# Causal attention with a quantised side product on one core: the order of a round's work changed on every engine

## The reference, cut to what matters

```python
xn = _layernorm(x)                                  # x: (4, 1024, 128)
q, k, v = (split_heads(xn @ W) for W in (Wq, Wk, Wv))   # 16 heads of 64
w = softmax(q @ k.T / 64 + causal)                  # 1024 x 1024 per head
mask = clip((arange(1024) + span * 1024) / 33, 0, 1)
w = w * mask; w = w / (sum(w) + 1e-8)
attn = concat_heads(w @ v) @ Wo
xi = clip(round(xn / scale), -127, 127) * scale     # made finite
out = x + attn + xi @ (ternary - 1).T + bias
```

## Time and profile before

| what | value |
|---|---|
| median of 3 runs | 1007.33 us (1005.56 to 1009.34) |
| the profiled execution | 1003.91 us, span 1002.2 us |
| granted TensorE clock | 0.997 of full speed |
| TensorE (PE) | 981.3 us busy, 98% |
| VectorE | 768.3 us, 77% |
| GpSimd | 708.8 us, 71% |
| ScalarE | 451.3 us, 45% |

### The profile page before, as it was taken

One profiled execution on the slowest core, in us unless ns is written; L12 is line 12 of the kernel. 1 busy time (PEld: TensorE's weight loads), 2 busy tenths in 40 slices (PEclk: granted clock), 3 DMA queues, 4 the chain that ended last, 5 costly groups with the idle time before them and its releaser, 6 DMA issues.

```text
span 1002.2 us, 19150 instructions
## 1 busy us (share of the span) xinstructions
PE 981.3 (98%) x7081; PEld 631.0 (63%) x7081; DVE 768.3 (77%) x1734; ACT 451.3 (45%) x607; POOL 708.8 (71%) x650
## 2 busy tenths in 40 slices
PE   7799999999999999999999999999999999999997
PEld 3566666666665666666666666666666666666654
DVE  8778888878788888877767877777877777787752
ACT  4344454444454444454444454444454443454442
POOL 8666767667767668767767777667767667767673
PEclk9999999999999999999999999999999999999999
DMA  6000000000000000000000000000000000000000
GB/s 176 3 3 2 2 1 3 2 2 3 1 23 2 3 2 3 1 3 2 3 12 12 2 3 2 2 3 2 2 2 24 2 3 2 1 2 2 2 1 22
DMA packets 16117, 8.52 MB, mean 9 GB/s; under 512 B 5388, under 2 KB 15628, under 8 KB 16024
## 3 DMA queue, kind: packets, MB, share of 16 engines
q1 hardware_dynamic: 15416, 7.16, 2.7%
q10 hardware_dynamic: 608, 0.14, 0.1%
HBM read 4.33 MB, written 2.10 MB: 6 GB/s over the span
## 4 chain that ended last, share of the span: by engine, by line
PE 88%; DVE 8%; issue 2%; DMA 1%; ACT 1%; SPq 0%; DVEq 0%; ACTq 0%
PE ring L939 25%; PE pv L956 25%; PE ring L912 12%; PE beside L995 7%; PE beside L968 6%; PE ring L885 3%; PE ring L881 3%; PE ring L882 3%; DVE ring L732 2%; DVE v L718 2%; PE ring L899 1%; DVE beside L756 1%; PE beside L983 1%; PE beside L919 1%; PE ring L900 1%
## 5 line engine op out<-in xcount | busy, mean ns | idle before, releaser
L541 ACT ACTIVATE prob<-ring 128x1024 f32<-128x1024 f32 (+3 forms) x384 | 293.6, 810 | 348.2 <-PE ring L939 348.2
L475 POOL TENSOR_TENSOR psumd<-psumd,prob 128x512 f32<-128x512 f32 (+1 forms) x252 | 410.7, 1630 | 28.7 <-ACT prob L541 0.8
L732 DVE CUSTOM_DVE_ANT_0 ring<-ring,causal 128x128 f32<-128x128 f32 (+3 forms) x512 | 240.3, 517 | 96.4 <-PE ring L912 96.0
L939 PE MATMUL ring<-q,k 64*128 64x512 f32 (+3 forms) x2304 | 280.0, 347 | 3.9 <-DMA mrow<-maxrow 2.4
L956 PE MATMUL pv<-prob,v 128*64 128x512 f32 (+3 forms) x1536 | 267.2, 490 | 0.0
L448 POOL TENSOR_SCALAR_AFFINE_SELECT prob<-prob 128x256 f32<-128x256 f32 x256 | 107.0, 419 | 218.0 <-ACT prob L541 215.8
L939 PEld LDWEIGHTS ring<-q,k 64*128 64x128 f32 x2304 | 195.2, 185 | 39.4 <-DVE rowmax L732 5.7
L956 PEld LDWEIGHTS pv<-prob,v 128*64 128x64 f32 x1536 | 104.7, 137 | 153.6 <-issue 139.9
L736 DVE TENSOR_REDUCE rowmax<-ring 128x2 f32<-128x1024 f32 x128 | 151.4, 1222 | 4.7 <-PE ring L912 1.4
L471 POOL TENSOR_TENSOR psumd<-prob 128x768 f32<-128x768 f32 x64 | 134.8, 2106 | 23.1 <-ACT prob L541 18.3
L912 PE MATMUL ring<-k,q 64*128 64x512 f32 (+3 forms) x768 | 143.2, 408 | 5.4 <-ACT k L530 1.2
(11 more groups left out here) (112 smaller groups left out, 942.4 us busy)
## 6 DMA issues: line engine op xcount, KB each, us to landing
x_sb<-in_L_attn_query SPq DMA_DIRECT2D x4, 512.0 KB, 5.2
kext<-kext SPq DMA_DIRECT2D x128, 4.0 KB, 1.7
out<-x_sb SPq DMA_DIRECT2D x8, 256.0 KB, 2.5
mrow<-maxrow SPq DMA_DIRECT2D x64, 4.0 KB
xn_sb<-in_L_attn_Wv SPq DMA_DIRECT2D x1, 512.0 KB, 5.2
wo<-in_L_attn_Wo SPq DMA_DIRECT2D x1, 512.0 KB, 7.3
xn_sb<-in_L_attn_Wq SPq DMA_DIRECT2D x1, 448.0 KB, 3.5
xn_sb<-in_L_attn_Wk SPq DMA_DIRECT2D x1, 448.0 KB, 4.2
```

The source lines that it names most:

```text
L475: g.tensor_tensor(acc[:, :, lo:HALF], acc[:, :, lo:HALF], pr[:, :, lo:HALF], ALU.add).then_inc(acc_done, 1)
L541: a.activation(prob[n % NPROB][:, :, lo:HALF], ring[:, slot(f"S{t}", i), :, lo:HALF], ACT.Exp, scale=1.0 / DH).then_inc(exp_done, 1)
L732: last = v.tensor_tensor_reduce(out=ring[:, s, h, 0:n], in0=ring[:, s, h, 0:n], in1=causal[:, HALF - n:HALF], scale=1.0, scalar=MASKED, op ...
L939: last = t_.matmul(ring[:, s, h, lo:HALF], k[p][rows, keys], q[p][rows, cols], start=(at == 0), stop=(at == len(parts) - 1))
```

## The change

All four engines' lists are written in another order. On TensorE, S0 and D1- and G11- now come in this sequence right behind the projections, and M0 and M1 behind them; Y0 moves into the next round and stands ahead of V, Y1 behind V; S7 and S8 come earlier. On VectorE the quantisation step q moves from the middle of the round to its start, ahead of Qlo and Klo, and one pair later; X0, X1 and W move ahead of R0 and R1. GpSimd's L and A are interleaved in another way, ScalarE's ln1-, ex1- stand behind E0. The last round has lists of its own for TensorE and now for VectorE.

```diff
-PE_PLAN = ("T Q+ K+ X0 X1 W G11- M0+ M1+ S0 S1 S2 M2+ D1- M3+ S3 V+ S4 S5 M4+ S6 M5+ Y1- M6+ M7+ S7 D0 G3 "
-           "M8+ S8 S9 S10 M9+ Y0 M10+ M11+ S11 G7")
+PE_PLAN = ("T Q+ K+ X0 X1 W S0 D1- G11- M0+ M1+ S1 S2 S3 S4 M2+ M3+ Y0- V+ Y1- M4+ S5 S6 S7 M5+ D0 M6+ M7+ "
+           "S8 G3 M8+ S9 M9+ S10 S11 M10+ M11+ G7")
...
-PE_LAST = "T G11- S0 S1 S2 D1- S3 S4 S5 Y1- S6 S7 D0 G3 S8 S9 S10 Y0 S11 F1 G7 D1 G11 Y1"
+PE_LAST = "T S0 D1- G11- S1 S2 S3 S4 Y0- S5 Y1- S6 S7 D0 G3 S8 S9 S10 Y0 S11 F1 G7 D1 G11 Y1"
...
     if name == "q":
-        return i % PAIRS_OF_BATCH < PAIRS_OF_BATCH - 1
+        return i % PAIRS_OF_BATCH > 0
...
-            for name, i in walk(DVE_PLAN, DVE_FIRST):
+            for name, i in walk(DVE_PLAN, DVE_FIRST, DVE_LAST):
...
-                    quantise(i // NPB, i % NPB + 1)
+                    quantise(i // NPB, i % NPB)
```

More of the change, by code:

```diff
@@ L25 @@
 LAST = N_PAIRS - 1
-PE_PLAN = ("T Q+ K+ X0 X1 W G11- M0+ M1+ S0 S1 S2 M2+ D1- M3+ S3 V+ S4 S5 M4+ S6 M5+ Y1- M6+ M7+ S7 D0 G3 "
-           "M8+ S8 S9 S10 M9+ Y0 M10+ M11+ S11 G7")
[L38 to L41, removed]
+PE_PLAN = ("T Q+ K+ X0 X1 W S0 D1- G11- M0+ M1+ S1 S2 S3 S4 M2+ M3+ Y0- V+ Y1- M4+ S5 S6 S7 M5+ D0 M6+ M7+ "
+           "S8 G3 M8+ S9 M9+ S10 S11 M10+ M11+ G7")
+ACT_PLAN = "Z Qhi+ Khi+ X0 X1 E0 ln1- ex1- E1 E2 E3 E4 E5 E6 E7 ln0 ex0 E8 E9 E10 E11"
+DVE_PLAN = ("Tc Z q Qlo+ Klo+ X0 X1 W R0+ R1+ t1- u1- o1- R2+ Ya0- R3+ Vs+ R4+ Ya1- R5+ R6+ R7+ t0 u0 R8+ "
+            "o0 R9+ R10+ R11+ Rc+")
+POOL_PLAN = "L0 L1 L2 A0 L3 A1 A2 A3 A4 A5 A6 A7 L8 L9 A8 L10 A9 A10 L11 A11 B"
 PE_FIRST = ("Q+ K+ M0+ M1+ M2+ I0+ M3+ I1+ M4+ I2+ M5+ I3+ M6+ I4+ M7+ I5+ M8+ M9+ M10+ M11+ Q++ T+ "
@@ L46 @@
 ACT_FIRST = "xf0+ Qhi+ xf1+ Khi+ rest+ keys+ wv+ Qhi++ Khi++ E0+ E1+ E2+"
-PE_LAST = "T G11- S0 S1 S2 D1- S3 S4 S5 Y1- S6 S7 D0 G3 S8 S9 S10 Y0 S11 F1 G7 D1 G11 Y1"
+PE_LAST = "T S0 D1- G11- S1 S2 S3 S4 Y0- S5 Y1- S6 S7 D0 G3 S8 S9 S10 Y0 S11 F1 G7 D1 G11 Y1"
+DVE_LAST = "Tc q t1- u1- o1- Ya0- Ya1- t0 u0 o0 Ya0 t1 u1 o1 Ya1"
 POOL_LAST = "L0 A0 L1 A1 L2 A2 L3 A3 A4 A5 A6 L8 L9 L10 A7 L11"
```

## The result

The changed kernel takes 1043.02 us in the median of 4 runs, the kernel before 1006.67 beside it. The ratio is 1.0367, with a 95% interval of 1.0343 to 1.0391: 36 us slower, where I had said 18 and a range up to 1034. The profiled execution took 1042.16 us, with a span of 1040.4. That span is 38.2 longer than before's, and this is the number that the trace can take apart.

The account below looks back on a forecast made before the run. TensorE, busy for 98% of the span, was taken as the bound. Plain rounds +9.6, D1 behind X +9.2, W in round 1 +1.1, early rounds -3.0 and ends +1.4 made +18.3 on 1007.33: 1025 us, range 1012 to 1034.

Parts of the forecast that it names:

- Switches: TensorE's changes of shape between units: 14 per round before, 11 after, saving 0.60 us per plain round.
- loads: TensorE weight loads not ahead of their unit, as behind a wait for a ring slot: 0.11 us more each.
- mrow: S0 follows the projections at once and waits for the two DMAs behind T: 0.36 us added per plain round.
- late slots: S2, S3, S4, S8, S10, S11 and M10 on TensorE get ring slots or loads late: 1.29 us added per plain round.
- plain round: A round without layer norm or X, T to T: 29.69 us before, 30.01 forecast, +9.6 in 30 rounds.
- the old waits: TensorE waits of M4, M2 and M9 in the old order that go: 0.73 us saved per plain round.
- rival 3: GpSimd's sums (A11) reach D1 late; ending 0.5 us late costs 15 over 30 rounds: 1040 us, chance 0.10.
- D1 behind X: In rounds 4, 5, 12, 13, 20 and 21 D1 waits for VectorE's read of X0 or X1: +9.2 us.
- The ends: Round 0 loses a Y0 (-1.1 us), the last round gains it and waits for mrow (+2.5): +1.4 together.
- Early rounds: Round 2 and five others with layer norm lose their wait for Klo, as units needing it stand later: -3.0 us.

## Why the prediction was wrong

The direction and the mechanisms that I had named were right, the size was half of what was measured, and a wait that I had not named made the most of the difference.

- **Switches, loads, mrow, late slots: right as a sum.** The plain round was 30.01 in the forecast. With Rc's wait taken away it measured 30.04 to 30.07. The waits for mrow and for the slots of S2 and S3 are there one by one, to 0.02 us. The savings of 0.60 for three switches and 0.73 for the old waits were not measured each by itself; that they are right is shown only by the sum.
- **The step that failed is the last one of the plain round.** I let T follow G7 at once and gave Rc no term. It took 1.35, and T waited: 0.40 in each of 30 rounds, 12 of the 20 us that were missing. I had placed GpSimd's sums only against D1 (rival 3, where they were in time, since A11 ended at T+2.9), and never against VectorE. The trace of the kernel before had the sign of it: a maximum over 8 numbers lasting 0.65 and ending with GpSimd's sum.

  The Trainium skill (SBUF — State Buffer, "SBUF: two separate sides") says that VectorE and GpSimd share a pair of ports of SBUF (the memory that holds these tensors) under an exclusive lock: of a VectorE instruction with two SBUF inputs and a GpSimd instruction that reads SBUF, the one that starts first has the pair for its whole length, and the other is blocked. The trace agrees: Rc with two inputs ends 0.02 behind the sum, wherever in the sum it started, and takes 0.17 where it meets none; Rc with one input takes 0.17 inside a sum.
- **D1 behind X: right in kind.** D1 came at T+6.1 in rounds 13, 20 and 21, against 6.06 forecast, at 6.3 and 6.55 in rounds 4 and 5, against 7.05 and about 6.4, but at 8.38 in round 12. In round 4 I had taken the 2.95 of the four normalisations from before as theirs, but part of it was a wait for GpSimd's sums; with the new order it is 2.23. Round 12 cost 5.9 instead of 2.5: the same meeting of VectorE and GpSimd, and then the clock, which had no term in the sum.
- **The ends: too small.** From the last T to the end it took 5.1 more, where I had 2.5, for the low clock behind the 3 us of idle time. Round 0 gave back 1.5 instead of 1.1.
- **Early rounds: nearly right.** Rounds 2, 3, 9, 10 and 11, taken against the plain rounds of their own kernel, gave back 2.4 against 3.0.
- **The range.** It left out what GpSimd does to VectorE. The ends of my bounds were those of each wait that I knew, and a missing term has no bounds. That Rc in every round and a normalisation in round 12 would be held up by GpSimd was in no rival; the nearest, rival 3, had the right engine with the wrong place, and that its 1040 came near the measurement is chance.

Of the 19.9 us between forecast and trace, Rc has 12.0, round 12 about 3.0 and the ends 2.1. Of the remaining 2.8, the early rounds have 0.6 and round 30 (31.04) another 0.5; the rest is in pieces of less than a tenth to a few tenths per round. None of this was followed up.

## What to carry to other kernels

Where the bound engine is nearly always busy, an order can be priced by start-to-start distances of its units, and this held to 0.1 us over the 26 us from T to G7. But then follow every engine to the round's end, and look at each small instruction that lasts far longer than its size: it shows a resource that it waits for now, and the change decides what it waits for next. A unit that needs no ring slot is worth more as a filler ahead of a late slot than next to a unit of its own shape.

## What the runs showed of the hardware that I had not expected

- A VectorE maximum of 128x8 with two SBUF inputs lasted 0.29, 0.65 or 1.35 us in three kernels, always to 0.02 behind the end of the GpSimd sum that ran, and 0.17 where none ran; a reduction of 128x16 from one SBUF tensor lasted 0.17 in the middle of such a sum. Normalisations of 128x128 from SBUF to SBUF were held up as well: four took 2.95, 4.32 or 2.23, and the last of the 4.32 ended 0.09 behind GpSimd's addition of the bias.
- After 3.04 and 3.72 us of idle time TensorE's next 5 to 7 us ran at a mean granted clock of 0.60 to 0.65. Shorter idle times went either way. Behind 1.88 in round 5 of the changed kernel the clock stayed at 1.00; in the same round, behind 1.87 with GpSimd's order undone and behind 1.89 with the bias moved, it fell to half for over 3 us, and the round took 1.3 and 1.7 longer. Idle times of 1.2 to 1.6 ahead of D1 in rounds 4, 13, 20 and 21 of the changed kernel left it at 1.00.
- Two changes of shape fewer made the kernel before 1.7% slower (1.0174), since the unit that had stood between them filled the time of a late slot.
